# Second absorbed attention: probabilities and values as float16 high and low parts, turned by DMA transposes, low parts by GpSimd, outputs as three products

## The reference

```
def _L2_xattn_ref(hidden_q, kv_c, Wq, w_kc_q, w_kc_kv, W_qr, W_kr, Wo):
    q_hk = (hidden_q @ Wq.T).reshape(b, s, H, K)
    q_big = jnp.einsum('bshk,hkq->bshq', q_hk, w_kc_q)
    kv_rope = kv_c * cos[None] + _rotate_half(kv_c) * sin[None]
    q_r = jnp.einsum('bshq,hqr->bhsr', q_big, W_qr)
    k_r = jnp.einsum('bld,hdr->bhlr', kv_rope, W_kr)
    scores = jnp.einsum('bhsr,bhlr->bhsl', q_r, k_r)
    attn = jax.nn.softmax(scores, axis=-1)
    ctx_c = jnp.einsum('bhsl,bld->bhsd', attn, kv_rope)
    ctx_lat = jnp.einsum('bhsd,hkd->bshk', ctx_c, w_kc_kv)
    return ctx_lat.reshape(b, s, H * K) @ Wo.T
```

## Time and profile before

| | us |
|---|---|
| median of 3 runs | 1272.53 |
| the three runs | 1267.84 to 1272.7 |
| span of the profiled execution (first to last instruction) | 1269.1 |
| fold stage of the change (the third layer), PE from about | 618.5 to 660.7 |
| plain stage, PE from about | 660.7 to 722.5 |
| PE, DVE, ACT, POOL busy over the span | 1177.4, 878.3, 508.2, 378.7 |

### The profile page before, as it was taken

One profiled execution on the slowest core, in us unless ns is written; L12 is line 12 of the kernel. 1 busy time (PEld: TensorE's weight loads), 2 busy tenths in 40 slices (PEclk: granted clock), 3 DMA queues, 4 the chain that ended last, 5 costly groups with the idle time before them and its releaser, 6 DMA issues.

```text
span 1269.1 us, 21808 instructions
## 1 busy us (share of the span) xinstructions
PE 1177.4 (93%) x8429; PEld 771.4 (61%) x8429; DVE 878.3 (69%) x1718; ACT 508.2 (40%) x1141; POOL 378.7 (30%) x397
## 2 busy tenths in 40 slices
PE   6889999999889999999899989889999888899997
PEld 4664658999645666566566745554655565456665
DVE  3777976676676666666757797987666676766666
ACT  3423360111233333333353345653334343555553
POOL 1540215656303333333203420001333242233332
PEclk9889999999999999999999997999999989999999
DMA  4030141000054444445330000002443200344342
GB/s 147 2 158 21 49 142 40 1 1 2 11 212 121 117 117 116 117 117 121 105 144 1 18 1 1 2 2 81 121 119 111 65 18 1 90 120 121 120 126 84
DMA packets 41544, 97.19 MB, mean 77 GB/s; under 512 B 5446, under 2 KB 18246, under 8 KB 39392
## 3 DMA queue, kind: packets, MB, share of 16 engines
q1 hardware_dynamic: 41440, 95.79, 24.8%
HBM read 94.35 MB, written 1.42 MB: 75 GB/s over the span
## 4 chain that ended last, share of the span: by engine, by line
PE 75%; DVE 14%; ACT 4%; issue 3%; DMA 2%; POOL 1%; SPq 0%; DVEq 0%; POOLq 0%; ACTq 0%
PE PS L1445 9%; PE PS L1446 9%; PE PS L1447 9%; PE PS L1490 4%; PE PS L1492 4%; PE PS L1491 4%; PE PS L1063 3%; PE PS L1081 2%; PE PS L1258 2%; PE PS L1049 2%; PE PS L1051 2%; PE PS L1050 2%; ACT arena L2286 2%; PE PS L2209 1%; DVE small L569 1%
## 5 line engine op out<-in xcount | busy, mean ns | idle before, releaser
L1670 POOL TENSOR_TENSOR arena<-arena,m_g 128x512 f32<-128x512 f32 x142 | 182.1, 1284 | 405.8 <-DMA m_g<-gate_rows 227.2
L1445 PE MATMUL PS<-arena 128*128 128x512 f16 x608 | 231.0, 380 | 3.5 <-DVE arena L1605 3.0
L1447 PE MATMUL PS<-arena 128*128 128x512 f16 x608 | 231.1, 380 | 0.0
L1446 PE MATMUL PS<-arena 128*128 128x512 f16 x608 | 231.1, 380 | 0.0
L1490 PE MATMUL PS<-arena 128*128 128x256 f16 x608 | 165.8, 273 | 11.7 <-DVE arena L1625 8.9
L1492 PE MATMUL PS<-arena 128*128 128x256 f16 x608 | 165.7, 273 | 0.0
L1491 PE MATMUL PS<-arena 128*128 128x256 f16 x608 | 165.7, 273 | 0.0
L1565 ACT ACTIVATE arena<-PS 128x512 f32<-128x512 f32 x112 | 66.8, 597 | 234.8 <-PE PS L1447 224.4
L1608 DVE SCALAR_TENSOR_TENSOR arena<-arena,PS 128x512 f32<-128x512 f32 x112 | 76.9, 686 | 120.0 <-ACT arena L1565 119.5
L1625 DVE TENSOR_TENSOR arena<-arena 128x512 f16<-128x512 f32 x142 | 112.4, 791 | 3.2 <-ACT arena L1575 3.2
L1447 PEld LDWEIGHTS PS<-arena 128*128 128x128 f16 x608 | 59.6, 98 | 72.1 <-issue 0.6
(11 more groups left out here) (282 smaller groups left out, 2250.1 us busy)
## 6 DMA issues: line engine op xcount, KB each, us to landing
w_stage<-in_up SPq DMA_DIRECT2D x80, 256.0 KB, 2.8
m_g<-gate_rows SPq DMA_DIRECT2D x70, 256.0 KB, 4.2
arena<-in_heads SPq DMA_DIRECT2D x16, 1088.0 KB, 5.3
w_stage<-in_down SPq DMA_DIRECT2D x80, 128.0 KB, 4.0
m_g<-gate_rows SPq DMA_DIRECT2D x17, 512.0 KB, 3.9
m_g<-gate_rows SPq DMA_DIRECT2D x6, 448.0 KB, 4.3
m_g<-gate_rows SPq DMA_DIRECT2D x6, 384.0 KB, 4.0
m_g<-gate_rows SPq DMA_DIRECT2D x6, 320.0 KB, 4.3
```

Of the source, the lines that this page charges most:

```text
L1445: pe.matmul(to, w_hi, x_hi, start=(k == 0), stop=False)
L1446: pe.matmul(to, w_lo, x_hi, start=False, stop=False)
L1447: ins = pe.matmul(to, w_hi, x_lo, start=False, stop=(k == KT - 1))
L1670: pool.tensor_tensor(m_c[:, st % 2, :], m_b[:, st % LAG, :], m_g[:, st // 2 % 2, st % 2, :], ALU.mult).then_inc(s.c, 1)
```

## The change

In the plain stage the probabilities and the folded values become pairs of float16 parts (a high part, and the rest as a low part, both scaled by 64), and the output is made as three float16 products, as the scores already are. The transposes leave PE: SP issues one DMA transpose for each event, which turns both parts (128 by 1024 of 2 bytes) from `plain_parts` to `plain_pt`. ACT no longer copies transposes from PSUM but makes the high part; GpSimd makes the low part, and a small multiplication of the reciprocals by 64 before its multiplication of the probabilities. PE's output comes 4 steps behind its scores instead of 3, and DVE's addition to `x` two steps later than before. In the fold stage ACT writes the high part of the folded values, and DVE gets two instructions a pair for the low part. DVE's maximum of event n waited for the transpose of n-4; it now waits for GpSimd's low part of n-4. Some semaphores are shared between the layers, which moves no instruction.

```
@@ act_fold2, dve_fold2
-                act.activation(fold_f[:, c::2, q, :], PS[:, (5, 7)[c], :]..., ACT.Copy).then_inc(s.f, 1)
+                act.activation(plain_f[:, 0, c::2, q, :], PS[:, (5, 7)[c], :]..., ACT.Copy, scale=SPLIT).then_inc(s.fh, 1)
+            def values_low(q):
+                for c in range(2):
+                    dve.wait_ge(s.fh, 2 * q + c + 1)
+                    dve.scalar_tensor_tensor(plain_f[:, 1, c::2, q, :], PS[:, (5, 7)[c], :]..., SPLIT,
+                                             plain_f[:, 0, c::2, q, :], ALU.mult, ALU.subtract).then_inc(s.f, 1)
+            values_low(0)
             for q in range(1, PAIRS):
...
+                values_low(q)
@@ new: SP
+        PLAIN_LAG = 4
+        def turns_landed(n):
+            return (s.turn0, s.turn1)[n % 2], 16 * (n // 2 + 1)
+        def sp_plain():
+            for n in range(4 * B):
+                b, half, q = plain_event(n)
+                sp.wait_ge(s.lo, n + 1)
+                if n >= 2:
+                    sp.wait_ge(*turns_landed(n - 2))
+                if b:
+                    sp.wait_ge(soft.y_ps, 2 * NT + QT * (b - 1) + q + 1)
+                sp.dma_start_transpose(plain_pt[n % 4]..., plain_parts[n % 4]...).then_inc(turns_landed(n)[0], 16)
@@ pe_plain
-            def transposed(n): ...
             def output(n):
                 b, half, q = plain_event(n)
-                pe.wait_ge(soft.t, PLAIN_0 + n + 1)
+                pe.wait_ge(*turns_landed(n))
                 if half == 0:
                     if b:
                         pe.wait_ge(soft.x, 2 * NT + QT * (b - 1) + q + 1)
...
-                    ins = pe.matmul(PS[:, (5, 7)[q], 0:D], plain_pt[q][:, j * P:(j + 1) * P], fold_f[:, b, j, :], ...)
+                    pe.matmul(to, p_hi, f_hi, start=(half == 0 and j == 0), stop=False)
+                    pe.matmul(to, p_hi, f_lo, start=False, stop=False)
+                    ins = pe.matmul(to, p_lo, f_hi, start=False, stop=(half == 1 and j == 3))
...
-            for n in range(1, 4 * B + 3):
+            for n in range(1, 4 * B + PLAIN_LAG):
                 if n < 4 * B:
                     scores(n)
-                if 2 <= n < 4 * B + 2:
-                    transposed(n - 2)
-                if n >= 3:
-                    output(n - 3)
+                if n >= PLAIN_LAG:
+                    output(n - PLAIN_LAG)
@@ act_plain (in place of evacuated; still called as high(n - 2) behind exponential(n))
+            def high(n):
+                act.wait_ge(norm.pn, PLAIN_NORM_0 + n + 1)
+                if b:
+                    act.wait_ge(*turns_landed(n - 4))
+                act.activation(plain_parts[n % 4][:, 0, :], plain_half(q, half), ACT.Copy).then_inc(s.hi, 1)
@@ pool_plain
+            def low(n):
+                pool.wait_ge(s.hi, n + 1)
+                pool.tensor_tensor(plain_parts[n % 4][:, 1, :], plain_half(q, half), plain_parts[n % 4][:, 0, :],
+                                   ALU.subtract).then_inc(s.lo, 1)
             for n in range(4 * B):
                 pool.wait_ge(soft.sums, PLAIN_0 + n + 1)
+                me.link(pool, pool.tensor_scalar(scaled, inverse, SPLIT, None, ALU.mult))
-                pool.tensor_tensor(p, p, over(small[:, q, 2, 8 * half:8 * half + 8], 2, L), ALU.mult).then_inc(norm.pn, 1)
+                pool.tensor_tensor(p, p, over(scaled, 2, L), ALU.mult).then_inc(norm.pn, 1)
+                if n:
+                    low(n - 1)
+            low(4 * B - 1)
@@ dve_plain
                 if n >= 4:
-                    dve.wait_ge(soft.t_ps, PLAIN_0 + n - 3)
+                    dve.wait_ge(s.lo, n - 3)
...
-                dve.tensor_tensor(tile, tile, PS[:, (5, 7)[q], 0:D], ALU.add).then_inc(soft.x, 1)
+                dve.scalar_tensor_tensor(tile, PS[:, (5, 7)[q], 0:D], UNSPLIT, tile, ALU.mult, ALU.add).then_inc(soft.x, 1)
...
-            for n in range(1, 4 * B + 4):
+            for n in range(1, 4 * B + 6):
                 if n < 4 * B:
                     softened(n)
                     summed(n)
-                if n >= 6 and n % 4 >= 2:
-                    added((n - 6) // 4, n % 2)
+                if n >= 8 and n % 4 < 2:
+                    added((n - 8) // 4, n % 2)
@@ the program on SP
             sp_first_chunk(2)
+            sp_plain()
             sp_ffn(2)
```

More of the change, by code:

```diff
@@ L180, in build @@
         plain_p, _ = take(8192, [2, 1024])
-        plain_pt = [take(a, [1024])[0] for a in (10240, 13312)]
+        plain_parts = [take(a, [2, 512], F16)[0] for a in (14336, 14848, 12288, 12800)]
+        plain_pt = [take(a, [2, 4, P], F16)[0] for a in (10240, 10752, 13312, 13824)]
         plain_x, _ = take(16384, [2, KT, NT, P], F16)
@@ L1236, in scores @@
                 ins.then_inc(s.s, 1)
-            def transposed(n):
-                b, half, q = plain_event(n)
-                pe.wait_ge(norm.pn, PLAIN_NORM_0 + n + 1)
-                if n >= 2:
-                    pe.wait_ge(soft.t, PLAIN_0 + n - 1)
-                else:
-                    pe.wait_ge(s.m, PAIRS)
-                for j in range(4):
-                    ins = pe.transpose(PS[:, n % 2, j * P:(j + 1) * P], plain_half(q, half)[:, j * P:(j + 1) * P], ident[:])
-                ins.then_inc(soft.t_ps, 1)
             def output(n):
                 b, half, q = plain_event(n)
-                pe.wait_ge(soft.t, PLAIN_0 + n + 1)
+                pe.wait_ge(*turns_landed(n))
                 if half == 0:
@@ L1256, in output @@
                         pe.wait_ge(s.f, 2 * PAIRS)
-                for j in range(4 * half, 4 * half + 4):
-                    ins = pe.matmul(PS[:, (5, 7)[q], 0:D], plain_pt[q][:, j * P:(j + 1) * P], fold_f[:, b, j, :],
-                                    start=(j == 0), stop=(j == PAIRS - 1))
+                for j in range(4):
+                    p_hi, p_lo = (plain_pt[n % 4][:, a, j, :] for a in range(2))
+                    f_hi, f_lo = (plain_f[:, a, b, 4 * half + j, :] for a in range(2))
+                    to = PS[:, (5, 7)[q], 0:D]
+                    pe.matmul(to, p_hi, f_hi, start=(half == 0 and j == 0), stop=False)
+                    pe.matmul(to, p_hi, f_lo, start=False, stop=False)
+                    ins = pe.matmul(to, p_lo, f_hi, start=False, stop=(half == 1 and j == 3))
                 if half:
@@ L1292, in act_plain @@
                 if n >= 2:
-                    evacuated(n - 2)
+                    high(n - 2)
             act_up_hi(2, 0)
```

91 lines of the change are left out of this document (49 added, 42 removed).

## The result

The changed kernel takes 1289.5 us in the median of 4 runs (1286.2 to 1294.9) and the kernel before 1271.0 on the same chip (1267.8 to 1272.7, 4 runs). The ratio is 1.0161, with a 95% interval of 1.0134 to 1.0189: slower by 1.3 to 1.9%. The profiled execution is the longest of the four: 1294.9 us with a span of 1293.1.

The account below looks back on a forecast made before the run. PE bounds the stage, with the DVE-ACT loop 0.5 us a step behind. Steps 9.3, late start 0.4, end 4.3, fold 0.6 and clock 3.0 make 17.6 us: span 1269.1 to 1286.7, plus 3.4 forecasts 1290; range 1279 to 1316.

Parts of the forecast that it names:

- The circle: Plain stage: scores, DVE event, addition to x, output, next scores in series; four steps 5.93 us, not 2.95: 11.9 us.
- the transfers' loop: Plain stage: DVE's subtraction via float16 parts, transfer, output and scores to a maximum five events later; 16.6 us against 14.75.
- The clock: PE's pauses in the plain stage halve its clock afterwards; 1.5 us for each of two long pauses, 3.0 us.
- The end that counts six pauses: Upper end of the clock loss in the plain stage, charging six PE pauses: 9 us.
- The transfers: Plain stage: each 256 KB DMA transpose lands in 4.2 us, with ends of 2.8 and 8.7.
- The two waits of 1.7 us: Plain stage: DVE waits 1.7 us at event 5 and at event 8, for transfers 0 and 3; 3.4 us.
- Slow transfers: Rival: plain-stage transfers near 8.7 us, ending 37 us late (1309), or 91 late (1364) if serial; 13 in 100.
- The tail: Plain stage, last maximum to last output: 13.4 us against 9.15, 4.3 more.
- GpSimd, ACT, DVE: Plain stage: GpSimd's 2.4 us an event hide under 2.95; ACT 0.63 + 0.58 as before, DVE's addition 0.38.
- The fold: Fold stage: DVE's low parts fill its idle time but delay PE's values, 0.6 us; first maximum 0.4 late.
- Not slower: Rival: additions reach x before PE needs the bank, circle stays open, DVE's pace rules; +2.0 us, 1274.5; 7 in 100.
- The clock that stays low: Rival: PE's clock stays low in the plain stage, 41 us late (1314), or 25 (1299) with clock between; 12 in 100.

Follow-up runs that it names:

- Experiment 1: The changed kernel with DVE's additions to x one event earlier; 1272.7 us, ratio 1.0024 to the kernel before.
- experiment 5: The kernel before, with only DVE's additions, factors and tokens one event later; 1288.5 us, ratio 1.0158 to the kernel before.
- experiment 2: The changed kernel with filler matmuls on PE ahead of the outputs that wait; 1281.8 us, ratio 1.0091 to the kernel before.
- Experiment 7: The changed kernel with additions and high part one event earlier, GpSimd's low part ahead of its scaling, and some PE filler matmuls; 1271.3 us, ratio 1.0030.
- experiment 4: The changed kernel with DVE's additions and ACT's high part both one event earlier; 1272.5 us, ratio 1.0021 to the kernel before.
- experiment 6: The changed kernel's float16 form with transposes on PE instead of DMA, additions where the kernel before has them; 1274.1 us, ratio 1.0045.

## Why the prediction was right

The forecast was 1290, with 1279 to 1316 as the range; the time is 1289.5. Step by step:

**The circle: right in mechanism, place and count.** Steps 9, 10, 13 and 14 are the long ones and no others; DVE idles for the scores and PE for L1365. Experiment 1 takes the circle out and 16.7 us go; experiment 5 puts it into the old kernel and 18.1 us come. Its size at full clock is 6.25 where the sum had 5.93 (experiment 2): four times 0.3 us are the handovers from engine to engine (3.51 us of PE's idle are DVE's event and addition with them, not 2.95 + 0.38), which I had left out of this term though not out of the transfers' loop. The term was 11.9, and is 13.2.

**The clock: the step that was mis-sized.** I charged the two long pauses, 3.0 us, and kept 9 as an end. It was 8.9 (experiment 2). The pause in each of the four circles, 3.5 to 3.9 us, was also followed by a clock of 0.50, and the burst behind it, 2.6 us at full clock, was wholly or half at half speed: against 6.25 the four steps are 1.6, 2.5, 1.3 and 1.7 longer, together 7.1; steps 5 to 8 make up the rest. The row I had taken, has a pause of two us and more, and the same fall; nothing in it excused the pauses of 3.3 us. The end that counts six pauses gave the right number, but not for the right pauses: the one before output 12, in the tail, cost nothing (12.17 for 12.13 in experiment 2), and the others cost 1.8 each and not 1.5. And that every pause costs is not a rule either, as experiment 5 shows.

**The transfers: right side, smaller.** They land in 3.1 us, near the lower end of 2.8 and not at 4.2. The Trainium skill's page "Advanced Engine Details and Errata", section "X-Bar Transpose (TRN2)", has them "as fast as regular DMAs", and the trace agrees: 3.1 us for 256 KB, between the 2.9 and the 4.2 of this trace's two ordinary loads of 256 KB. The Trainium skill's page "VectorE: DVE Perf Modes", section "The three transpose paths", gives 1309 ns for a tile of 128 by 128; eight in a row would be an estimate of 10.5 us, and the trace, with 3.1, shows nothing of the kind. The two waits of 1.7 us (steps 5 and 8, 4.65 each by the sum) came as 6.19 and 3.92 with the clock in them, and as 4.04 and 4.26 (steps 5 and 6) at full clock: 2.4 us in all for the 3.4 of the sum. Slow transfers, the second rival, are excluded; the wait at the first output was there, but short.

**The tail:** 3.0 more, for 4.3. The faster transfer, 3.1 for 4.2, would give 1.1 of the difference.

**GpSimd, ACT, DVE.** The groups of the changed kernel in the stage:

```profile
L1336 POOL TENSOR_TENSOR arena<-arena,small 128x512 f32<-128x512 f32 x16 | 16.7, 1043 | 1.3
L1334 POOL TENSOR_SCALAR small<-small 128x8 f32<-128x8 f32 x16 | 3.7, 233 | 44.1 <-DVE small L1360 44.1
L1327 POOL TENSOR_TENSOR arena<-arena 128x512 f16<-128x512 f32 x16 | 18.4, 1155 | 31.5 <-ACT arena L1310 31.5
L1310 ACT ACTIVATE arena<-arena 128x512 f16<-128x512 f32 x16 | 9.7, 614 | 2.1 <-POOL arena L1336 2.1
L1365 DVE SCALAR_TENSOR_TENSOR x<-PS,x 128x256 f32<-128x256 f32 x8 | 3.1, 390 | 0.6 <-PE PS L1285 0.6
```

The small multiplication takes 0.23 us for the 0.30 from the slope, the low part 1.16 between the taken 1.04 and the end of 1.28, the addition 0.39 for 0.38. GpSimd's 2.4 us an event hide, as said.

**The fold:** 0.6 and 0.4 were taken; from the feed-forward's last additions to the first maximum it is 46.5 us before and 46.9 after, so 0.4 for both. The low parts do fill DVE's idle time of the earlier trace rows:

```profile
644.61 0.76 DVE L1009 SCALAR_TENSOR_TENSOR arena<-PS,arena 128x256 f16<-128x256 f32 x2 [0.78 <-ACT arena L975]
645.29 1.28 DVE L990 SCALAR_TENSOR_TENSOR arena<-PS,arena 128x512 f16<-128x512 f32 x2
646.76 0.29 DVE L997 COPY arena<-PS 128x128 f32<-128x128 f32 x1 [0.19 <-PE PS L873]
```

1.39 us of idle before the copy became 1.28 of work and 0.19 of idle, and in these pairs PE's values come every 5.46 us for 5.39 before. The wait that the prediction put at 0.15 us in each of four pairs came instead once, in the second pair, and longer (L885 are the values, the old L880):

```profile
630.98 1.09 PE L885 MATMUL PS<-arena,kvr 64*64 64x256 f32 x16 [1.56 <-DVE arena L990]
```

It adds nothing to the 46.9: experiments 2 and 7 have no such wait there, but a clock of 0.86 from 618 to 630 as in the kernel before, and take 46.9 as well. It is a risk all the same. In experiment 4's profile the same wait, 1.55 us, was followed by the low clock, and the way took 51.7.

**The sum.** Predicted 17.6 on the span; the medians differ by 18.5, and in the profiled execution the stage is 21.2 longer. The clock's 5.9 and the circle's 1.3 that were missing are partly paid by the tail (1.3), the waits (1.0) and the fold (0.6). The profiled execution is 5.4 us above its median, and its span of 1293.1 at a clock of 0.966 stands beside spans of 1284.4 to 1288.5 at 0.968 to 0.974 in the other three, so part of the surplus is that execution's own. I had set the kernel before at 1272.5, the median shown, and with one run more it is 1271.0: 1.5 too high, against 0.9 too little for the change. So the 0.5 us of error in the forecast is less than its terms earned: misses of both signs met, and that is luck.

**The rivals.** Not slower: its point of decision was whether the addition is over when scores 8 are. It isn't: scores 8 end at 693.9, and the addition starts at 696.91. Experiments 1 and 4 are that rival built: 1.0024 and 1.0021, or 4.1 and 4.0 us above the 1268.5 of the kernel before, where it had given +2.0. The clock that stays low (1299 to 1314): it holds for the circles, where the clock fell behind each of the four pauses, but not between them, where it returned to 1.00. This rival was nearer to the truth in its mechanism than the 12 in 100 it got.

## What to carry to other kernels

When work is moved to later events on one engine, write down the waits that meet there and look for a closed circle: the output waits for the addition, the addition stands behind an event, the event waits for scores that stand behind the output. Its price is the sum of everything in it and not the longest part, and one event of slack opens it again. A pause that such a circle makes on TensorE can be paid a second time in the clock of the burst behind it. Here the clock cost 8.9 us beside 13.2, while in experiment 5 three pauses of 3.07 us out of five cost no clock; so give the forecast two ends, one with every pause counted and one with none. And taking work off the bounding engine gives only the distance to the next serial loop (0.5 us a step by the sum). Experiment 7 had 3.6 us over 15 steps, since DVE's additions stand in that loop too, and its longer chain to the last result took the same 3.6 back.

## What the runs showed of the hardware that I had not expected

A DMA transpose of 128 by 1024 float16 (256 KB) from SBUF to SBUF lands 3.1 us after its issue and holds SP's queue for 1.23 us, though the 16 of them move in 16,896 packets, all under 512 B. TensorE's clock fell to 0.50 after each of four pauses of 3.5 to 3.9 us in the changed kernel, at once in two of them and 0.7 and 1.3 us later in the others, and after only two of five pauses of 3.07 us in experiment 5. It stayed at 1.00 throughout where filler matmuls left PE 63.1 busy of 72.4 us. In experiment 6, with a pause of half a microsecond in each step, the clock stayed at 1.00 too.
